# Softmax attention: GpSimd adds the probabilities of two masked key tiles, and one product sums both

## The reference

```python
q = embedded @ Wq.T + bq ; k = embedded @ Wk.T + bk ; v = embedded @ Wv.T + bv   # 2 batches, 16 heads of 8
qk = jnp.einsum('bhqd,bhkd->bhqk', q, k) / jnp.float32(np.sqrt(s))
p = jax.nn.softmax(qk, axis=-1)
mask = jnp.triu(jnp.ones((s, s), dtype=p.dtype), k=0)
p = p * mask
z = jnp.einsum('bhqk,bhkd->bhqd', p, v)
```

## Time and profile before

| | us |
|---|---|
| median of three timed runs | 879.54 (878.7 to 881.68) |
| the profiled execution | 875.54 |
| its span, first to last instruction | 873.7 |
| TensorE busy, matmuls | 670.2 |
| VectorE busy | 580.2 |
| ScalarE busy | 454.7 |
| GpSimd busy | 330.9 |

### The profile page before, as it was taken

One profiled execution on the slowest core, in us unless ns is written; L12 is line 12 of the kernel. 1 busy time (PEld: TensorE's weight loads), 2 busy tenths in 40 slices (PEclk: granted clock), 3 DMA queues, 4 the chain that ended last, 5 costly groups with the idle time before them and its releaser, 6 DMA issues.

```text
span 873.7 us, 14331 instructions
## 1 busy us (share of the span) xinstructions
PE 670.2 (77%) x4582; PEld 344.9 (39%) x4582; DVE 580.2 (66%) x1141; ACT 454.7 (52%) x872; POOL 330.9 (38%) x767
## 2 busy tenths in 40 slices
PE   4275867645308947799999999999999999951993
PEld 4162322534307944123333434343333423421893
DVE  5426999724633448778787787879978798333343
ACT  2045611224105635047877677867768677851661
POOL 0635564155442432321433324144342444171242
PEclk9996999568558978559999999999999999995897
DMA  8352940035112013620020202020020000011103
GB/s 265 110 147 50 286 69 1 9 110 136 29 40 83 30 55 108 186 66 2 17 40 2 56 1 57 1 57 1 2 56 2 1 2 2 1 37 48 55 29 100
DMA packets 56929, 51.31 MB, mean 59 GB/s; under 512 B 6152, under 2 KB 46804, under 8 KB 56600
## 3 DMA queue, kind: packets, MB, share of 16 engines
q1 hardware_dynamic: 52168, 42.19, 18.4%
q0 software_dynamic: 4544, 7.60, 3.3%
q10 hardware_dynamic: 144, 0.61, 0.2%
HBM read 30.04 MB, written 21.80 MB: 59 GB/s over the span
## 4 chain that ended last, share of the span: by engine, by line
PE 54%; issue 18%; DVE 15%; DMA 5%; SPq 2%; ACT 2%; POOL 2%; another core or an unknown queue 0%; ACTq 0%; POOLq 0%; DVEq 0%
PE PS L1076 14%; PE PS L1004 11%; PE PS L1043 11%; DVE ARENA L1817 6%; PE PS L781 5%; PE PS L792 5%; DVE X L1422 2%; PE PS L744 2%; DMA ARENA<-slots_x 2%; PE PS L753 2%; PE PS L731 2%; DVE XN L1373 2%; DVE STATS L1346 1%; POOL slots_x L1871 1%; SPq L540 1%
## 5 line engine op out<-in xcount | busy, mean ns | idle before, releaser
L1817 DVE TENSOR_REDUCE ARENA<-PS 128x1 f32<-128x1024 f32 x256 | 300.8, 1218 | 62.5 <-PE PS L1004 61.8
L1311 ACT ACTIVATE ARENA<-PS 128x512 f32<-128x512 f32 x512 | 273.0, 607 | 79.0 <-PE PS L1043 73.9
L1004 PE MATMUL PS<-ARENA 72*128 72x512 bf16 x512 | 164.6, 405 | 13.5 <-DMA ARENA<-k_parts 7.1
L1043 PE MATMUL PS<-ARENA 75*128 75x512 bf16 x512 | 162.5, 384 | 1.7 <-issue 1.7
L1076 PE MATMUL PS<-ARENA 128*8 128x128 f32 (+8 forms) x1920 | 151.4, 430 | 1.2 <-POOL ARENA L1993 0.9
L1993 POOL TENSOR_SCALAR_AFFINE_SELECT ARENA<-ARENA 128x128 f32<-128x128 f32 x256 | 73.9, 296 | 127.8 <-ACT ARENA L1311 127.4
L1043 PEld LDWEIGHTS PS<-ARENA 75*128 75x128 bf16 x512 | 47.8, 98 | 90.3 <-ACT ARENA L1311 38.6
L1004 PEld LDWEIGHTS PS<-ARENA 72*128 72x128 bf16 x512 | 42.7, 99 | 98.2 <-DVE ARENA L1817 38.5
L1692 DVE TENSOR_TENSOR ARENA<-PS,ARENA 128x512 f32<-128x512 f32 x46 | 31.8, 692 | 65.5 <-PE PS L781 65.5
L1076 PEld LDWEIGHTS PS<-ARENA 128*32 128x32 f32 (+2 forms) x1920 | 43.2, 97 | 76.8 <-issue 41.7
L1901 POOL DMA_INDIRECT tokens_y<-ARENA x46 | 44.6, 970 | 74.4 <-DVE ARENA L1701 72.3
(11 more groups left out here) (188 smaller groups left out, 878.7 us busy)
## 6 DMA issues: line engine op xcount, KB each, us to landing
ARENA<-pack_dram SPq DMA_DIRECT2D x8, 514.0 KB, 12.7
ARENA<-slots_x SPq DMA_DIRECT2D x16, 256.0 KB, 4.0
slots_y<-ARENA SPq DMA_DIRECT2D x32, 128.0 KB, 2.8
ARENA<-q_parts SPq DMA_DIRECT2D x21, 192.0 KB
ARENA<-k_parts SPq DMA_DIRECT2D x21, 192.0 KB
slots_x<-FILL SPq DMA_DIRECT2D x2, 1483.5 KB, 18.4
ARENA<-slots_x SPq DMA_DIRECT2D x10, 258.0 KB, 5.1
k_parts<-ARENA SPq DMA_DIRECT2D x10, 256.0 KB, 3.7
```

Of the source, the lines that this page charges most:

```text
L1004: ins = nc.tensor.matmul(PS[:, slot + c, :], Q3[0:KQ, G % Q3R, g, i * P:(i + 1) * P], K3[0:KQ, G % Q3R, g, c * 512:(c + 1) * 512], start=T ...
L1043: nc.tensor.matmul(PS[:, bank, 0:w], K3[0:MR + 3, G % Q3R, i, j * P:(j + 1) * P], Q3[0:MR + 3, G % Q3R, i, half * 512:half * 512 + w], sta ...
L1311: nc.scalar.activation(PT[:, n % NPT, 0:w], PS[:, bank_of[x], 0:w], ACT.Exp).then_inc(b_exp, 1)
L1817: nc.vector.tensor_reduce(NM[:, k % 4, i:i + 1], PS[:, slot:slot + 2, :].rearrange("p b n -> p (b n)"), AX.X, ALU.max, negate=True).then_i ...
```

## The change

GpSimd adds, in place, the probabilities of steps 8 and 9, and of 10 and 11, in groups 0 to 6 (`MERGES` holds the second step of each pair; 14 pairs). The products of these 28 steps are taken out of the plan; for each pair one product "D" sums the added probabilities, after the last B two steps behind the pair's second step. The product of step 12 comes in the middle of step 14, ahead of that of step 13 at its usual place. The last group keeps its products. The ring `PT` grows from three steps to five (eight of its buffers lie where weights of the first blocks were), `MD` keeps its 12 buffers, and GpSimd now waits for the product of step k-3 before it writes a masked copy. Score tiles are counted by themselves and spread to two in every step; splits go with them, and the turn M of most units from the fifth pair on comes after the next unit's split, two score tiles later than before. Waits that counted products count them by the new order (`products_through`).

```diff
@@ constants @@
-NPT = 12
+NPT = 20
+NPA = 12
+NMD = 12
...
+MERGES = [G * NS + st for G in range(GR - 1) for st in (TB + 1, TB + 3)]
+MERGED = set(MERGES) | {m - 1 for m in MERGES}
+SUMMED = 2
@@ attention_turns @@
+def late(unit):
+    return unit[0] >= 4 and unit[0] % 4 != 3 and unit != (4 * GR - 2, 1)
...
+    for u, (hh, h) in enumerate(units):
         for n, i in enumerate(tiles_of_unit(h)):
             turns.append(("A", hh, i))
...
+            if n == SI and u >= 1:
+                turns.append(("S", *units[u - 1]))
+            if n == SI and u >= 2 and late(units[u - 2]):
+                turns.append(("M", *units[u - 2]))
+            if n == MI and u >= 1 and not late(units[u - 1]):
+                turns.append(("M", *units[u - 1]))
@@ attention_plan @@
-            want = ahead + -(-rest * (4 * m + g + 1) // (4 * (steps - AEND)))
...
-                want = max(want, turns.index(("M", 4 * G + 3, s // TB)) + 1 + LEAD)
-            while at < min(want, len(turns)):
+            tiles = taken + -(-rest * (4 * m + g + 1) // (4 * (steps - AEND)))
+            want = turns.index(("M", 4 * G + 3, s // TB)) + 1 if g == 0 and s in (0, TB) else 0
+            while at < len(turns) and (at < want or turns[at][0] != "A" or done < tiles):
...
+            if g == 1 and m - VD - 2 in MERGES and m - VD - 1 not in MERGED:
+                plan.append(("V", m - VD - 1, 0))
             if m >= VD and g == VG:
-                plan.append(("V", m - VD, 0))
+                if m - VD not in MERGED and m - VD - 1 not in MERGES:
+                    plan.append(("V", m - VD, 0))
+                if m - SUMMED in MERGES:
+                    plan.append(("D", MERGES.index(m - SUMMED), 0))
@@ TensorE @@
+                    elif kind == "D":
+                        m = MERGES[k]
+                        G, st = divmod(m, NS)
+                        if st == TB + 1:
+                            pe.wait_ge(z_copied, 2 * G + 1)
+                        pe.wait_ge(den_added, 4 * (k + 1))
+                        for g in range(4):
+                            ins = nc.tensor.matmul(PS[32 * g:32 * g + 32, 7, :], ONE8, probs_of(4 * m + g),
+                                                   start=(st == TB + 1), stop=False, skip_group_check=True)
                         ins.then_inc(pv_done, 1)
@@ ScalarE, exponentials @@
-                            act.wait_ge(pv_done, k - NPT // 4 + 1)
+                            act.wait_ge(pv_done, products_through(k - NPT // 4))
@@ GpSimd @@
+                        n = 4 * k + i
+                        if k in MERGES:
+                            pool.wait_ge(b_exp, n + 1)
+                            nc.gpsimd.tensor_tensor(probs_of(n), probs_of(n), probs_of(n - 4), ALU.add
+                                                    ).then_inc(den_added, 1)
                         if diag is None:
                             continue
...
                         pool.wait_ge(b_exp, n + 1)
-                        nc.gpsimd.affine_select(out=MD[:, n % NPT, :], in_=PT[:, n % NPT, diag:diag + P],
+                        if k >= NMD // 4:
+                            pool.wait_ge(pv_done, products_through(k - NMD // 4))
+                        nc.gpsimd.affine_select(out=MD[:, n % NMD, :], in_=probs_of(n)[:, diag:diag + P],
```

## The result

The changed kernel takes 903.3 us (median of four, 900.4 to 905.9) against 879.1 for the kernel before (876.8 to 881.7): 1.029 times as long, 95% interval 1.025 to 1.033. The direction was foretold; the size was not: +24 us, where +8 was forecast and the range ended at 895. A difference in us is such a ratio less one, times the median of the kernel before, unless medians are named; brackets behind a ratio are its 95% interval.

A forecast was written before the change was run, and what follows sets the result against it. TensorE was taken to set the pace, except in groups 4 and 6, where VectorE does. +0.4 (groups 0, 1, 2, 3, 5), +3 (group 4) and +4.5 (group 6) gave +7.9 on 879.54: 887.4 us, range 877 to 895.

The forecast's parts named there:

- VectorE's limit: Steps without a product: reductions 1.13 us apart hold up score tiles, so at most 0.8 of 2.2 us a group is kept.
- the add's price: Each of 56 GpSimd adds occupies 1.21 us, from a 1265 ns row; range 1.10 to 1.30.
- the chain in the clean groups: From the product of step 7 to the second D: 12.2 us in groups 2 and 5, set by GpSimd's adds and splits.
- The ring of five steps: Buffers of probabilities: costs nothing, since exponentials never wait for it before or after.
- the even spread of the tiles: Score tiles over the steps: worth nothing where TensorE is full, since their number is the same.
- the clean groups: Groups 0, 1, 2, 3 and 5: TensorE's saving turns into waits for GpSimd at D; +0.4 us together.
- the port: Group 4: VectorE's two-input operations and GpSimd adds wait out each other's whole instruction; +3 us, bounds 0 and 6.
- Group 6: Inverse roots between the adds lengthen GpSimd's chain, 3.8 us, plus 0.7 for writes of normed rows; +4.5 us.
- D finds its adds done: Sign that the prediction is wrong: the joint product would not wait for GpSimd's adds.
- Adds hidden: Rival: adds end ahead of each D and VectorE alone limits; needs a chain under 11.4 us; 875.5 us, chance 0.12.
- Even: Rival: group 4's operations miss the adds, slack takes up group 6's roots, 0 to 2 us remain; 880.5 us, chance 0.17.
- Likeliest: GpSimd's queue decides at each second D, with the roots and the port adding to it; chance 0.68.

The follow-up runs named there:

- the plan alone: Changed kernel with no pair merged (all 128 products, no adds), keeping ring, tile spread and splits; 1.0022 of the kernel before.
- the filled kernel: Changed kernel with matmuls that nobody reads put into TensorE's waits in groups 4 and 6; median 897.4 us against 880.6, ratio 1.014.
- the kernel with the pause of 2 adds: Kernel before, with the product of step 8 of group 2 made to wait once for two unread GpSimd adds; ratio 1.0072.
- The clean groups by themselves: Changed kernel with pairs merged only in groups 0, 1, 2, 3 and 5; 1.0079 of the kernel before, +6.9 us.
- groups 4 and 6 by themselves: Changed kernel with pairs merged only in groups 4 and 6; 1.0248 of the kernel before, +21.8 us.

## Why the prediction was right in its direction and wrong in its size

**Right: VectorE's limit.** At most 0.8 us of a group's 2.2 could be kept; 0.7 to 0.8 were without the adds, in groups 0, 2, 3 and 5. In group 1 it was 0.1.

**Right: the add's price, and the chain in the clean groups.** The trace has a line for the adds of each pair of places in memory (shortest, median, longest ns); these are three of the four:

```profile
L2044 POOL TENSOR_TENSOR ARENA<-ARENA x24: 1259/1265/1286, 418.8 to 743.1; 128x512 f32<-128x512 f32 x24
L2044 POOL TENSOR_TENSOR C<-C x12: 1255/1264/1277, 413.0 to 680.6; 128x512 f32<-128x512 f32 x12
L2044 POOL TENSOR_TENSOR C<-C,ARENA x8: 1263/1271/1317, 519.4 to 617.1; 128x512 f32<-128x512 f32 x8
```

That is the earlier trace rows's 1265 ns. The single adds of 1.6 us that were to show beside VectorE did not come, the longest took 1.317: it was VectorE that waited. The estimate of 1.12 us from the Trainium skill's figure (GPSIMD Engine Reference, section 3.1) was too low by this measurement. The chain took 12.4 us in group 5 (foretold 12.2) and 13.1 in group 1 (12.7). D waited for GpSimd 0.96 us in group 0, 0.96 and 0.43 in group 1, 0.27 and 0.64 in group 2, 0.26 and 0.51 in group 5, where 0.1 to 0.7 and near 0.8 were foretold. The ring of five steps and the even spread of the tiles are worth nothing that can be told from no change (the plan alone).

**A term too small: the clean groups.** +0.4 foretold, +4.6 measured. 1.8 are in group 0, with 3.4 us of half clock behind the first D; 1.4 in group 1 (about 0.4 of them in the plan alone too), 0.9 in group 5. In groups 3 and 5 M waits 0.7 and 0.5 us behind the second D for a split queued behind the masks. The prediction had it that "the wait of VectorE disappears inside it", the wait at D; but VectorE gets no tile while TensorE waits at D, and its own limit may well come on top. That is argued and not shown, and how much belongs to each was not taken apart.

**Group 4, at full clock: as foretold, with some luck.** +3 for the port, the middle of bounds of 0 and 6 for two sets of four operations; 25.5 in the filled kernel is 2.6 above the 22.9 of before and 3.3 above the plan alone. One set met the adds, the other (at 620.4 in the earlier trace rows, at 629.50 in the changed kernel) missed them and took 1.18 us. The timeline of the changed kernel is that of the earlier trace rows's operations:

```profile
613.41 5.04 POOL L2044 TENSOR_TENSOR C<-C,ARENA 128x512 f32<-128x512 f32 x4
615.17 3.69 DVE L1514 SCALAR_TENSOR_TENSOR X<-XNT,RSTD,X 128x128 f32<-128x128 f32 x4
...
620.18 1.04 PE L1045 MATMUL PS<-ARENA 72*128 72x512 bf16 x2 [3.57 <-DVE ARENA L1868]
...
623.28 1.94 PE L1128 MATMUL PS<-C,ARENA 128*32 128x512 f32 x8
```

Four operations of 1.13 us took 3.69, and each of the first three ended just behind an add. The first row of TensorE shows what the prediction did not price: the wait of 3.57 us, and the matmuls behind it at 1.2 GHz.

**Group 6, at full clock: too small, and by another path.** +4.5 foretold; 29.3 in the filled kernel is 7.6 above the 21.7 of before and 6.7 above the plan alone. Of the 4.5, 3.8 were to come because GpSimd's queue ends too late for the second D. It did not: the last add ended at 744.32 and D started at 749.13, without a wait, and in the filled kernel too its adds were done 3.4 us ahead. "D finds its adds done" was the prediction's own sign of being wrong. The roots between the adds are there, but what waited for them was VectorE, 3.07 us before the writes of the normed rows. The port on those writes was the small term, 0.7 taken of bounds 0 to 3.5, and it came to 3.8:

```profile
739.40 4.92 POOL L2044 TENSOR_TENSOR ARENA<-ARENA 128x512 f32<-128x512 f32 x4
739.49 4.92 DVE L1424 TENSOR_SCALAR XN<-X,MV,RSTD 128x128 f32<-128x128 f32 x4 [3.07 <-POOL RSTD L2010]
...
745.60 1.03 PE L1045 MATMUL PS<-ARENA 72*128 72x512 bf16 x2 [4.00 <-DVE ARENA L1868]
```

The same four writes in the trace of before:

```profile
720.90 1.11 DVE L1373 TENSOR_SCALAR XN<-X,MV,RSTD 128x128 f32<-128x128 f32 x4
```

Both engines show 4.92 us, one instruction of each in turn. TensorE then waited 4.00 us for the maxima that stood behind the writes.

**The step that failed: a wait of TensorE was priced at its length.** The prediction read the granted clock as 1.00 in the earlier trace rows and held it there. The change takes work away from TensorE in that stage and puts waits in its place, and in most kernels with such waits the 1.00 went in groups 4 and 6, in part of them in group 0 as well; a single pause of 4.54 us did it too, one of 2.1 us did not in its profile. The filled kernel sizes the missing term: 9.1 us in group 4 and 5.1 in group 6, 14.2 in all, and 0 in the sum. The 29.0 of the 30.5 us between the profiles thus split into 4.6 (clean) + 2.6 (group 4) + 7.6 (group 6) + 14.2 (clock). Without the last term 14.8 are left where 7.9 were foretold: the direction was no luck, and 879.5 + 14.8 = 894.3 us would still lie in the range, so it is the clock that carried the time out of it. The profile of the kernel before had shown that the clock can fall: its mean is 0.881, and in the blocks ahead of the attention, where TensorE is not full, the slices hold 5 to 9.

**The rivals.** "Adds hidden" fell on the chain (it wanted less than 11.4 us and got 12.4); the kernel with the adds left out in the clean groups is that rival made real, and its gain of 5.5 us [3.5, 7.6] covers the 4.0 that the rival gave. "Even" fell: the operations of group 4 met the adds, and nothing took up the roots of group 6. "Likeliest" had GpSimd's queue decide at each second D. It did in groups 1, 2 and 5; in groups 4 and 6, which hold most of the loss, TensorE waited for VectorE and never for an add.

**What stays open.** What brings the clock down is not shown, only that it fell where TensorE had gaps and did not where they were filled. Whether it falls at a given wait differs from run to run and from kernel to kernel (group 0 and the kernel with the pause of 2 adds above), so the share of it in the timed runs is known from the means alone. The clean groups by themselves and groups 4 and 6 by themselves add to 28.7 us, all together measured 25.6 by the ratio; the intervals cover that. No version that computes the whole reference was found to beat the kernel before; shorter adds, or an order in which the adds stand further ahead of D, were not tried.

## What to carry to other kernels

Work may be taken off a full TensorE only if what is next in line is faster by more than that work: otherwise the gain comes back as TensorE's waits, and in groups 4 and 6 such waits were charged twice, once as time and once as half clock. When a stretch shows a granted clock of 1.00, ask what keeps it there before pricing a wait at its length. Work that is moved to GpSimd is priced by what runs on VectorE beside it: next to free beside reductions, but beside GpSimd's adds VectorE's two-operand operations, and its `TENSOR_SCALAR`, took 3.3 and 4.4 times as long. And follow the wait to its end: what GpSimd delays on VectorE can reach TensorE through the next tile, and not where the two engines meet in the plan.

## What the runs showed of the hardware

- The clock of TensorE fell to half behind waits that are short one by one (0.96 us in group 0; 1.26 us in group 6, in three kernels; once 0.84 in the kernel with a pause of 2 adds), and stayed full behind a single wait of 2.1 us in one profile. Half clock lasted 3.4 us in one run and 20.5 in another after the same work.
- At half clock a TensorE that was otherwise full lost 6.3 us in 13.65, and being full (20.23 busy of 20.48 us) did not end it sooner.
- A VectorE `TENSOR_SCALAR` of 128x128 float32 with scalars from memory is held up by GpSimd adds (4.92 us for four instead of 1.11), and by GpSimd's constant fills as well (4.33 us, the first of the four waiting out all eight fills). Four `SCALAR_TENSOR_TENSOR` of that size took 3.69 us beside adds and 1.13 beside fills.
